# Experts' down projections as one fp32 matmul each instead of three on split operands, with three product buffers and a lag of two units

## The reference

```python
x = layernorm(x + attention(x, Wq, bq, Wk, bk, Wv, bv, Wo, bo))   # 16 heads of 8
# feed-forward on xf = x.reshape(2048, 128)
shared_out = silu(xf @ sw1) * (xf @ sw3) @ sw2                    # 256 hidden
s = sigmoid(xf @ router_w.T)
topk_idx = top_k(s + router_bias, 2)
gates = s_sel / (denom + 1e-09)                                   # of the 2 chosen
h = gelu(einsum('nd,edh->neh', xf, ew1))                          # 8 experts, 128 hidden
y = einsum('neh,ehd->ned', h, ew2)
routed_out = einsum('ned,ne->nd', y, comb)                        # comb: gate per token and expert
x = layernorm(x + shared_out + routed_out)
```

## Time and profile before

| | us |
|---|---|
| runs | 265.13, 265.02, 263.12 |
| median | 265.02 |
| span of the profiled execution | 261.9 |
| PE busy | 225.9 (86%) |
| DVE busy | 186.1 (71%) |
| ACT busy | 152.3 (58%) |
| POOL busy | 119.1 (45%) |

### The profile page before, as it was taken

One profiled execution on the slowest core, in us unless ns is written; L12 is line 12 of the kernel. 1 busy time (PEld: TensorE's weight loads), 2 busy tenths in 40 slices (PEclk: granted clock), 3 DMA queues, 4 the chain that ended last, 5 costly groups with the idle time before them and its releaser, 6 DMA issues.

```text
span 261.9 us, 4502 instructions
## 1 busy us (share of the span) xinstructions
PE 225.9 (86%) x1546; PEld 158.7 (61%) x1546; DVE 186.1 (71%) x370; ACT 152.3 (58%) x292; POOL 119.1 (45%) x186
## 2 busy tenths in 40 slices
PE   1766984999999999994999999997999899999850
PEld 1434854667677677772676766655767576767520
DVE  8953893777969879794269762348567796976953
ACT  1440722576666667663356678866696468665620
POOL 8677381000100007130448988435319977273511
PEclk9995885899999999999589999999979999999995
DMA  7277864405528082476000000069980495792111
GB/s 191 53 92 91 86 69 98 40 11 86 45 53 77 23 85 30 78 53 228 3 0 5 3 5 5 4 108 140 226 143 28 94 147 84 129 161 74 40 40 40
DMA packets 16198, 19.43 MB, mean 74 GB/s; under 512 B 1280, under 2 KB 11712, under 8 KB 16032
## 3 DMA queue, kind: packets, MB, share of 16 engines
q1 hardware_dynamic: 15744, 18.49, 43.4%
q0 software_dynamic: 144, 0.39, 1.0%
q10 hardware_dynamic: 288, 0.27, 0.6%
HBM read 11.22 MB, written 1.11 MB: 47 GB/s over the span
## 4 chain that ended last, share of the span: by engine, by line
PE 59%; DMA 13%; DVE 11%; POOL 6%; issue 5%; ACT 3%; SPq 1%; POOLq 0%; DVEq 0%; ACTq 0%
PE ring L818 17%; PE pv_bank L832 14%; PE max_bank L804 12%; DMA kstack<-gate_scratch 6%; DMA qstack<-top_rows 4%; POOL qstack L522 3%; DVE kstack L629 3%; DVE probs_mem L737 2%; DMA kstack<-qk_parts 2%; ACT qstack L556 1%; PE misc_bank L871 1%; PE misc_bank L882 1%; PE max_bank L788 1%; PE max_bank L789 1%; PE max_bank L790 1%
## 5 line engine op out<-in xcount | busy, mean ns | idle before, releaser
L669 DVE TENSOR_REDUCE top<-max_bank 128x2 f32<-128x512 f32 x128 | 84.0, 684 | 32.9 <-PE max_bank L804 31.7
L569 ACT ACTIVATE probs_mem<-ring 128x512 f32<-128x512 f32 x128 | 73.9, 597 | 43.6 <-PE ring L818 42.4
L818 PE MATMUL ring<-qstack,kstack 128*128 128x256 f32 x256 | 62.9, 331 | 7.7 <-DMA qstack<-top_rows 7.7
L818 PEld LDWEIGHTS ring<-qstack,kstack 128*128 128x128 f32 x256 | 40.5, 199 | 35.9 <-ACT probs_mem L569 25.1
L804 PE MATMUL max_bank<-kstack,qstack 128*128 128x256 f32 x256 | 56.5, 312 | 3.6 <-DMA kstack<-qk_parts 3.3
L804 PEld LDWEIGHTS max_bank<-kstack,qstack 128*128 128x128 f32 x256 | 43.0, 209 | 7.7 <-DMA kstack<-qk_parts 4.1
L832 PE MATMUL pv_bank<-probs_mem,v 128*18 128x256 f32 x512 | 41.3, 397 | 0.0
L737 DVE TENSOR_TENSOR probs_mem<-probs_mem,kstack 128x512 f32<-128x512 f32 x32 | 24.8, 798 | 11.9 <-POOL qstack L522 6.2
L556 ACT CAST qstack<-probs_mem 128x512 fp32r<-128x512 f32 x32 | 19.7, 615 | 16.5 <-DVE probs_mem L737 16.2
L522 POOL TENSOR_TENSOR qstack<-probs_mem,qstack 128x512 fp32r<-128x512 f32 x14 | 19.5, 1392 | 16.2 <-ACT qstack L556 16.1
L473 POOL TENSOR_SCALAR rstd<-mv 128x2 f32<-128x2 f32 x8 | 1.8, 226 | 48.7 <-DVE mv L706 48.5
(11 more groups left out here) (146 smaller groups left out, 386.6 us busy)
## 6 DMA issues: line engine op xcount, KB each, us to landing
kstack<-gate_scratch SPq DMA_DIRECT2D x4, 2048.0 KB, 15.5
kstack<-qk_parts SPq DMA_DIRECT2D x24, 64.0 KB
wf<-w_ffn_dram SPq DMA_DIRECT2D x1, 1408.0 KB, 5.8
qstack<-qk_parts SPq DMA_DIRECT2D x9, 128.0 KB
xs<-x_dram SPq DMA_DIRECT2D x4, 256.0 KB, 5.2
out_dram<-xs SPq DMA_DIRECT2D x4, 256.0 KB, 2.3
kstack<-wf_hi SPq DMA_DIRECT2D x12, 64.0 KB
qstack<-wf_hi SPq DMA_DIRECT2D x6, 128.0 KB
```

The source lines that it names most:

```text
L569: nc.scalar.activation(probs[:, k // 2 % 4, c % 2 * 512:(c % 2 + 1) * 512], ring[k % NRING][:, :], ACT.Exp, scale=SCALE).then_inc(probs_ma ...
L669: dve.tensor_reduce(top[:, half, h:h + 3:2], max_bank[n % NMAX][:, :].rearrange("p (h k) -> p h k", h=2), AX.X, ALU.max).then_inc(max_take ...
L818: ins = mm(ring[k % NRING][:, j * S:(j + 1) * S], kstack[:, s, ab, r, kt * P:(kt + 1) * P], qstack[:, s, r, :], start=True, stop=True)
```

## The change

The experts' down products are no longer three fp32r matmuls on split operands but one fp32 matmul of the unsplit weight columns of `wf` and the gated product itself. So the experts' `hi_part` and low parts, the buffers `hid_hi` and `hid_lo` and the job "last parts" are gone, and GpSimd splits only the first 1792 columns of the weights, in 16 pieces of 112. The gated product has three buffers instead of two; expert unit m's product waits for the down product of unit m - 3, and TensorE's down product for the gated product. LAG is 2: each down product and all that follows it in the lists stands one tick earlier. The shared units keep their split; their product waits for the low part of three units earlier.

```diff
@@ -39,12 +39,14 @@
 NSH = 2
+NHB = 3
...
+SPLIT = 512 + NE * P + 256
...
-        wf_lo = qk_parts[:, :, :].rearrange("p g t -> p (g t)")[:, 0:RW]
+        wf_lo = qk_parts[:, :, :].rearrange("p g t -> p (g t)")[:, 0:SPLIT]
...
-        hid_hi = qstack[:, 0, :, :].rearrange("p r q -> p (r q)").rearrange("p (n t) -> p n t", n=4)
-        hid_lo = qstack[:, 1, :, :].rearrange("p r q -> p (r q)").rearrange("p (n t) -> p n t", n=4)
...
-        act_out, hid, acc_t = ffn[:, 0:2, :], ffn[:, 2:4, :], ffn[:, 4, :]
...
+        act_out, hid, acc_t = ffn[:, 0:2, :], ffn[:, 2:2 + NHB, :], ffn[:, 5, :]
...
-        LAG = 3
+        LAG = 2
...
-        jobs[UP0 + NHID, 0].append(("last parts", 0))
...
-            if n < NG * NSH:
-                g, j = divmod(n, NSH)
-                return sh_hi[:, j, tokens(g)], sh_lo[:, j, tokens(g)]
-            return hid_hi[:, n % 4, :], hid_lo[:, n % 4, :]
+            g, j = divmod(n, NSH)
+            return sh_hi[:, j, tokens(g)], sh_lo[:, j, tokens(g)]
...
-            return n % 2 == 0 or n in (NG * NSH - 1, NG * NSH + 1, NHID - 1)
+            return n % 2 == 0 or n == NG * NSH - 1
...
-            cuts = [slice(c, c + RW // PIECES) for c in range(0, RW, RW // PIECES)]
-            assert cuts[-1].stop == RW
+            cuts = [slice(c, c + SPLIT // PIECES) for c in range(0, SPLIT, SPLIT // PIECES)]
+            assert cuts[-1].stop == SPLIT
...
-                    if kind == "hidden" and not lo_by_dve(n):
+                    if kind == "hidden" and n < NG * NSH and not lo_by_dve(n):
                         pool.wait_ge(hi_made, n + 1)
                         hi, lo = hidden_parts(n)
-                        pool.tensor_tensor(lo, hid[:, 1, :], hi.bitcast(F32), ALU.subtract).then_inc(lo_made[1], 1)
+                        pool.tensor_tensor(lo, hid[:, n % NHB, :], hi.bitcast(F32), ALU.subtract).then_inc(lo_made[1], 1)
...
-                m = n - NG * NSH
                 act.wait_ge(hid_made, n + 1)
-                if m >= 4:
-                    act.wait_ge(down_made, m - 3)
-                nc.scalar.copy(hidden_parts(n)[0], hid[:, n % 2, :]).then_inc(hi_made, 1)
+                nc.scalar.copy(hidden_parts(n)[0], hid[:, n % NHB, :]).then_inc(hi_made, 1)
...
-                        if b:
+                        if 0 < b <= NG * NSH:
                             hi_part(b - 1)
-                    if kind == "last parts":
-                        hi_part(NHID - 1)
...
                         dve.wait_ge(act_made, b + 1)
-                        if b >= 2:
-                            dve.wait_ge(lo_made[b % 2], b // 2)
+                        n = b - NHB
+                        if 0 <= n < NG * NSH:
+                            dve.wait_ge(lo_made[n % 2], n // 2 + 1)
                         m = b - NG * NSH
+                        if m >= NHB:
+                            dve.wait_ge(down_made, m - NHB + 1)
...
-                        dve.tensor_tensor(hid[:, b % 2, :], act_out[:, b % 2, :], other, ALU.mult).then_inc(hid_made, 1)
-                        if b and lo_by_dve(b - 1):
+                        dve.tensor_tensor(hid[:, b % NHB, :], act_out[:, b % 2, :], other, ALU.mult).then_inc(hid_made, 1)
+                        if 0 < b <= NG * NSH and lo_by_dve(b - 1):
                             lo_part(b - 1)
-                    if kind == "last parts":
-                        lo_part(NHID - 1)
...
                         n = NG * NSH + b
-                        pe.wait_ge(lo_made[n % 2], n // 2 + 1)
-                        c = slice(E2 + e * P, E2 + (e + 1) * P)
-                        three(acc, wf_hi[:, c], wf_lo[:, c], hid_hi[:, b % 4, :], hid_lo[:, b % 4, :],
-                              False, e == NE - 1).then_inc(down_made, 1)
+                        pe.wait_ge(hid_made, n + 1)
+                        mm(acc, wf[:, E2 + e * P:E2 + (e + 1) * P], hid[:, n % NHB, :], start=False,
+                           stop=e == NE - 1).then_inc(down_made, 1)
```

More of the change, by code:

```diff
@@ L139, in build_layer @@
                  for i in range(2)]
-        hid_hi = qstack[:, 0, :, :].rearrange("p r q -> p (r q)").rearrange("p (n t) -> p n t", n=4)
-        hid_lo = qstack[:, 1, :, :].rearrange("p r q -> p (r q)").rearrange("p (n t) -> p n t", n=4)
         ffn = probs_mem[:, :].rearrange("p (n t) -> p n t", n=8)
-        act_out, hid, acc_t = ffn[:, 0:2, :], ffn[:, 2:4, :], ffn[:, 4, :]
[L144 to L147, removed]
+        act_out, hid, acc_t = ffn[:, 0:2, :], ffn[:, 2:2 + NHB, :], ffn[:, 5, :]
+        res2 = ffn[:, 6, :].rearrange("p (t d) -> p t d", t=TPG)
+        stats2 = ffn[:, 7, 0:6 * TPG].rearrange("p (t n) -> p t n", t=TPG)
+        mv2 = ffn[:, 7, 64:64 + 2 * TPG].rearrange("p (t n) -> p t n", t=TPG)
+        rstd2 = ffn[:, 7, 128:128 + TPG]
         ring = [ctx.enter_context(nc.psum_tensor(f"ring{i}", [P, 512], F32)) for i in range(NRING)]
@@ L653, in lo_part @@
                 hi, lo = hidden_parts(n)
-                dve.tensor_tensor(lo, hid[:, n % 2, :], hi.bitcast(F32), ALU.subtract).then_inc(lo_made[n % 2], 1)
+                dve.tensor_tensor(lo, hid[:, n % NHB, :], hi.bitcast(F32), ALU.subtract).then_inc(lo_made[n % 2], 1)
             dve.wait_ge(wa_loaded, 16)
```

## The result

| | before | after |
|---|---|---|
| median of the runs on one chip | 264.65 us (263.12 to 265.13, 4 runs) | 260.75 us (260.36 to 261.68, 4 runs) |
| span of the profiled execution | 261.9 | 258.0 |

The ratio is 0.9866, with a 95% interval of 0.982 to 0.9912: faster by 1.3%, 3.9 us, where 3.0 were predicted. The changed kernel's times fall into two groups, near 256 us at a mean granted clock of 0.967 and at 260 to 262 us at 0.93 to 0.955; all four of this set are of the second, two of four in a later set are of the first.

The account below looks back on a forecast made before the run. TensorE was nearly full, with 9.0 us of down-product waits for lo parts. Last matmul slot: 252.84 - 9.0 + 5.3 (fp32) + 0.7 (new waits) = 249.8, 3.0 earlier; span 258.9, median 3.1 above: 262.0 us, range 260.3 to 266.3.

Parts of the forecast that it names:

- rival 4: Expert stage, better than said: no new waits and some slow clock goes, -3.7 - 0.6, 260.7 us; chance 10%.
- The waits for lo parts: Expert stage: TensorE's down products wait 9.0 us for their lo parts; all of it was to go.
- a loop through the product's two buffers: Expert units: a product buffer comes free only when the lo part of two units earlier is made; next product waits.
- The fp32 product: Expert down products on TensorE: 0.864 us each, 0.165 more than the three matmuls replaced; times 32, +5.3 us.
- New waits: Expert stage: two or three of six blocks at 0.2 to 0.4 us each, 0.7 us added to the sum.
- the slow clock at 191 us: TensorE from 191.00 to 194.96: 1.7 us lost to slow clock, after idling for ScalarE's exp, untouched by the change.
- the start at 191: Up product of expert unit 1, at 191.00 us; a stage starting later than 191 would show the prediction wrong.
- Lag and buffers: Expert units: with lag two and three buffers, 3.1 us of TensorE work hides gelu, product and hand-overs; slack 1.5 us.
- The smaller split: GpSimd's weight split in the attention stage, pieces of 112 columns instead of 176: worth nothing, 0.3 us if a hidden wait exists.
- Part of the waits has another cause: Expert stage: VectorE late by other work and GpSimd's router steps; 4.5 to 8 of 9.0 go, middle 263.8 us; chance 25%.
- Lag two is too short: Expert down products: each of 32 waits 0.2 us for VectorE, 6.4 us lost, 267.7 us; chance 10%.
- Weight loads exposed by the change of kinds: TensorE, expert stage: 0.12 us at each of 64 changes between product kinds, +7.7, in all +4.7, 269.7 us; chance 5%.

Follow-up runs that it names:

- the second trace: The changed kernel run once more with no edit: median 258.27 us (256.09 to 261.05, 4 runs).
- the changed kernel with unread parts: Changed kernel, but the experts' hi and lo parts are made and not used, and all weight columns are split: 264.78 us, ratio to before 0.9958.
- the kernel with three matmuls: Changed kernel with three fp32r matmuls per down product, without hi and lo parts, reading the up weights (computes something else): 256.21 us, ratio to before 0.9731.
- the full split: Changed kernel, but GpSimd splits all 2816 weight columns in pieces of 176 instead of 112: median 261.19 us (256.51 to 261.82).

## Why the prediction was right

The change was forecast as 3.0 us faster, and 3.9 were measured. The median of 260.75 us lies 1.25 under the forecast, 0.15 under the forecast's own range (260.9 to 263.2) and beside rival 4 (260.7). The changed kernel's second set of runs, 258.27, lies outside the whole range of 260.3 to 266.3. So the mechanism of the sum is borne out below, but that the time fell inside the range was in part luck with the clock of the executions.

**The waits for lo parts, 9.0 us.** Right in size: none is left at a down product but 0.17 us ahead of down 24 and 0.26 in it, and in the second trace not even these. **Their cause was half right.** The prediction read the earlier trace rows as a loop through the product's two buffers. With a third buffer the kernel before kept TensorE's waits, with one more unit of lag besides it traded them for waits of finT, and the changed kernel with unread parts got 4.7 to 5.0 us back, as waits for products. That the parts cause the waits is shown. How they divide is not: the work on VectorE, its slower products beside GpSimd, the buffer that a lo part holds. The stages with parts on all units and a lag of three or four (59.7 to 60.6), and the 61.7 with unread parts, fit a limit outside TensorE, which takes in the 5.0 us of the fp32 product without getting much longer; this is an argument and no run isolates it. The chain of waits shows who came last each time; it did not tell that removing one link would only bring up the next.

**The fp32 product, 0.864 us.** Right: 0.86 in the chain above, 1.55 from down to down with an up of 0.70. That is 32 x 0.155 = 5.0 us where 5.3 stood in the sum. The timeline puts the next up matmul's start 0.45 us behind the product's and then takes 0.63 to its second step, so the price is read over a whole unit. The Trainium skill, "FP8 and Floating Point Precision", section "TensorE Precision Notes", counts four passes; at one 0.233 step each (0.93) they would have given 7.4. The trace does not agree with that reading; it does not show how many passes there are.

**New waits, 0.7 us.** Some 0.4 came in the first trace, all at unit 24 and so from the gate load, none from finT or norm2; none came in the second. The load was predicted to go out at 221.9 and to land at 237.3; it went out at 221.52, and the product behind it began at 237.51. TensorE was predicted at down 24 at 238.6; it was free for it at 238.08 and began at 238.25. That this load is nearly the second limit is confirmed by the kernel with three matmuls, which got 3.6 to 3.9 of 5 us.

**What the sum did not have.** It took the slow clock at 191 us (1.7) and the start at 191 as fixed. In the profiled execution after, the slow stretch was absent (-1.5) and the stage began 1.19 us later, which the prediction had named as a sign of being wrong. Both are the clock of the execution: for the first see the traces with lag 3 and with the full split; as to the second, the same matmul of attention starts at 133.36 us in both kernels, the granted clock stays at 0.50 until 133 us before and until 135 after, and behind that the changed kernel is 1.0 us late. The two nearly cancelled, which was luck: last down product over at 249.33 instead of 253.25, 3.9 earlier against the 3.0 predicted. By stages less their slow clock the change gave 3.6 to 3.9 us (60.6 to 57.0 and 56.7): the sum without its 0.7 of new waits, 3.7, was the nearer. This is rival 4, "better than said", in what happened.

**Lag and buffers.** Both put at nothing or a small risk. The lag is worth nothing here (56.7 with three) and was no risk; the third buffer holds about 1 us, which the prediction did not cost. The two were taken back one at a time; the changed kernel with lag three and two buffers was not run.

**The smaller split** was put at nothing, and is.

**The rivals.** "Part of the waits has another cause": the cause was in part other, yet the waits went with it, since it too came from the parts. Its evidence, L737 of up to 1.752 us, was real: the longest in the changed kernel is 0.802. "Lag two is too short" is true of a kernel with parts (69.7 and 65.1) and not of this one. Weight loads exposed by the change of kinds: 1.55 a unit leaves no room.

## What to carry to other kernels

An engine that looks like the bound by busy time can still be held up by helpers: count its work from start to start, and what is left over is what a costlier but simpler instruction may use up. When the precision trick (three matmuls on split operands) needs more work from the other engines than it saves on TensorE, one fp32 matmul at 0.86 us can beat three at 0.70, as here, and it also permits a shorter lag, which the split operands do not. To find out whether an engine's waits come only from its reading the helpers' results, make the work and don't read it; what stays is the work's own cost, with any buffer that it still holds.

## What the runs showed of the hardware

- An fp32 matmul of 128x512 costs 0.86 us at full clock as two records, 3.7 steps of an fp32r matmul of the same shape (0.233), also when it stands between fp32r ones.
- The same VectorE multiplication of two SBUF operands took 0.691 us as a mean in the changed kernel (at most 0.802), where GpSimd makes no lo parts of experts, and 0.744 to 0.893 in the five kernels where it makes 14 or 15 of them (at most 1.66 to 1.82). With half of the lo parts made, all on VectorE, it is 0.689 to 0.699: what costs is GpSimd's part of them. The Trainium skill, "SBUF — State Buffer", section "Who interferes with whom", says that such a pair contends; the trace agrees.
- The granted clock of TensorE fell or did not fall at the same instruction after the same idle time of 0.65 us: 0.53 against 1.00 at 192 us in two kernels that are alike there. It stayed low for a longer or a shorter time, 0.63 against 0.88 as a mean from 123 to 137 us, in two executions of one kernel after idle times of 4.86 and 4.43 us. The latter moved the start of the expert stage by 3.6 us, as much as the whole change is worth. A comparison of single executions has to be made stage by stage, with the clock beside it.
